# Making the queries of the second cross-attention for two tiles at once, in a loop body of sixteen steps

## The reference, cut to what matters

```python
B, S, D, H, DK, DV = (4, 256, 128, 16, 64, 64)
Q = (queries @ W_Q).reshape(b, sq, H, DK)
K = (keys @ W_K).reshape(b, skv, H, DK)
V = (values @ W_V).reshape(b, skv, H, DV)
scores = jnp.einsum('bqhd,bkhd->bhqk', Q, K)
scores = jnp.where(mask == 0, -jnp.inf, scores)
probs = jax.nn.softmax(scores * scaling, axis=-1)
attn = jnp.einsum('bhqk,bkhd->bqhd', probs, V).reshape(b, sq, H * DV)
return attn @ W_O
...
x = x + _L1_xattn_ref(_layernorm(x, axis=-1), ctx_1024, ctx_1024, mask_1x1xSxS2_ik0, ...)
```

## Time and profile before

| What | Value |
|---|---|
| median of 3 runs | 2666.25 us (2664.68 to 2667.53) |
| the profiled execution's own time | 2666.86 us |
| its span | 2665.0 us |
| TensorE busy | 2229.0 us, 84% of the span |
| VectorE busy | 1711.6 us, 64% |
| ScalarE busy | 1442.8 us, 54% |

### The profile page before, as it was taken

How to read it: one execution, slowest core, us unless ns; L and a number is a source line. 1 busy time by engine, 2 the same in 40 slices (tenths; PEclk the granted TensorE clock), 3 DMA queues, 4 the chain that set the end, 5 groups by cost and what they waited for, 6 DMA issues and landing times. The chain is left out here.

```text
span 2665.0 us, 80517 instructions
## 1 busy us (share of the span) xinstructions
PE 2229.0 (84%) x26087; PEld 1655.4 (62%) x26087; DVE 1711.6 (64%) x5620; ACT 1442.8 (54%) x3658; POOL 458.0 (17%) x1104
## 2 busy tenths in 40 slices
PE   5999999988759997999999999995357117499998
PEld 3777777767636665888888888884125103344444
DVE  4888888877654443777777777776789878701100
ACT  5888888876612223544554454453578747632221
POOL 2444444433213230000000000000000030000000
PEclk9999999999869997999999999998698555799999
DMA  3222222210100003444444444442000000100001
GB/s 92 75 73 73 73 73 73 73 38 1 26 0 0 0 0 92 113 109 106 113 109 104 106 116 104 108 110 71 0 0 0 0 1 4 45 0 0 0 0 32
DMA packets 257634, 140.91 MB, mean 53 GB/s; under 512 B 40176, under 2 KB 255616, under 8 KB 257152
## 3 DMA queue, kind: packets, MB, share of 16 engines
q1 hardware_dynamic: 257536, 139.61, 19.9%
HBM read 118.57 MB, written 20.97 MB: 52 GB/s over the span
## 5 line engine op out<-in xcount | busy, mean ns | idle before, releaser
L1075 DVE CUSTOM_DVE_ANT_0 c_SM<-c_bs,c_MB 128x257 f32<-128x257 f32 x512 | 211.1, 420 | 125.9 <-PE c_bs L979 124.2
L1052 ACT ACTIVATE c_OT<-c_bo 128x512 f32<-128x512 f32 x128 | 76.4, 597 | 389.5 <-PE c_bo L992 389.5
L979 PE MATMUL c_bs<-c_cT,c_QP 128*128 128x257 f32 x1024 | 264.1, 396 | 9.9 <-DVE c_LT L1094 9.9
L992 PE MATMUL c_bo<-c_PT,c_C 32*128 32x128 f32 x8192 | 266.0, 277 | 2.5 <-DVE c_PT L1090 2.3
L677 ACT ACTIVATE a_PR<-a_SM,a_nmx 128x257 f32<-128x257 f32 x512 | 253.4, 499 | 4.0 <-issue 3.3
L1046 ACT ACTIVATE c_PR<-c_SM,c_nmx 128x257 f32<-128x257 f32 x512 | 253.3, 504 | 0.0
L992 PEld LDWEIGHTS c_bo<-c_PT,c_C 32*128 32x128 f32 x8192 | 241.6, 187 | 18.6 <-issue 4.0
L979 PEld LDWEIGHTS c_bs<-c_cT,c_QP 128*128 128x128 f32 x1024 | 182.2, 190 | 56.6 <-issue 24.0
L724 DVE CUSTOM_DVE_ANT_0 a_SM<-a_bs,a_MB 128x257 f32<-128x257 f32 x512 | 187.9, 422 | 44.5 <-PE a_bs L545 38.6
L1090 DVE STREAM_TRANSPOSE c_PT<-c_PR 128x256 f32<-128x256 f32 x512 | 181.2, 411 | 0.0
L949 POOL TENSOR_TENSOR c_XL<-quarter,c_PR 128x16 f32<-128x16 f32 x128 | 27.6, 216 | 738.8 <-DVE c_PR L1085 738.8
(11 more groups left out here) (489 smaller groups left out, 4901.3 us busy)
## 6 DMA issues: line engine op xcount, KB each, us to landing
c_C<-in_ctx_dram SPq DMA_DIRECT2D x512, 128.0 KB, 2.8
a_C<-in_ctx_dram SPq DMA_DIRECT2D x128, 128.0 KB, 2.1
ctxT_dram<-a_cT SPq DMA_DIRECT2D x128, 128.0 KB, 1.9
c_cT<-ctxT_dram SPq DMA_DIRECT2D x128, 128.0 KB, 2.5
a_MK<-in_mask_Bx1xSxS_bk_dram SPq DMA_DIRECT2D x128, 32.1 KB, 1.9
X<-in_x_dram SPq DMA_DIRECT2D x4, 512.0 KB, 6.2
g_h<-in_L_ffn_h_w_dram SPq DMA_DIRECT2D x2, 1024.0 KB, 8.5
out_dram<-X SPq DMA_DIRECT2D x1, 2048.0 KB, 8.7
```

The costliest lines, as they stand in the source:

```text
L979: nc.tensor.matmul(b_s[hg][:, 0:SK], QP[:, r // 4 % 2, r % 4, 4 * hg:4 * hg + 4, :], cT[:, r, :], start=True, stop=True).then_inc(s_ps, 1)
L992: last = nc.tensor.matmul(b_o[:, h, 0:P], C[rows, buf, kb, :], PT[rows, s.r % 2, kb, :, :], start=(kb == 0), stop=(kb == NKB - 1), tile_po ...
L1075: nc.vector.tensor_tensor_reduce(SM[:, par, hg, :], b_s[hg][:, 0:SK], MB[:, :], 1.0, NEG1, ALU.add, ALU.max, mx[:, par, hg:hg + 1]).then_i ...
```

## The change

A pair of tiles (eight batches, 256 columns) takes the place of a tile in `queries`. A chunk is now two heads for a pair: 2 matmuls, 4 passes of 256 columns. Chunks alternate between banks 0 and 1 and banks 2 and 3 of `b_o`, in columns 128 to 383, and a chunk waits for the copy of the chunk before the last one, not of the last one. `QP` holds 2 x 8 batches in place of 2 x 4. There are still 128 chunks of 512 columns for ScalarE to copy; nine of them are made ahead of the steps, one in each step after that, and the last eight steps have none. The written-out steps are 16 at each end (with the three that finish), and the loop has 6 iterations of a body of 16 steps, on every engine; its branch is taken 5 times.

```diff
-        QP = sb("c_QP", [D, 2, BPT, H, SQ])
+        QP = sb("c_QP", [D, 2, 2 * BPT, H, SQ])
...
         def run(eng, step, extra):
 
-            def one(g, r, tile, fours, eights):
-                s = Step(g, r, B)
-                s.tile, s.fours, s.eights = tile, fours, eights
+            def one(g, r, first):
+                s = Step(g, r % 8, B)
+                s.fours, s.eights = (lambda lag: 4 * first + (r + lag) // 4), (lambda lag: 2 * first + (r + lag) // 8)
+                s.tile, s.side = s.fours(0), lambda lag: (r + lag) // 8 % 2
                 step(s)
-            for g in range(8):
-                one(g, g, g // 4, lambda lag, g=g: (g + lag) // 4, lambda lag, g=g: (g + lag) // 8)
-            with eng.Fori(1, B // 8 - 1) as j:
-                for r in range(8):
-                    one(8 * j + r, r, 2 * j + r // 4, lambda lag, j=j, r=r: 2 * j + (r + lag) // 4,
-                        lambda lag, j=j, r=r: j + (r + lag) // 8)
-            for g in range(B - 8, B + extra):
-                one(g, g % 8, g // 4, lambda lag, g=g: (g + lag) // 4, lambda lag, g=g: (g + lag) // 8)
+            for g in range(16):
+                one(g, g, 0)
+            with eng.Fori(1, B // 16 - 1) as j:
+                for r in range(16):
+                    one(16 * j + r, r, j)
+            for g in range(B - 16, B + extra):
+                one(g, g - (B - 16), B // 16 - 1)
...
-            def queries(tile, c, o_done):
-
-                wait(pe, q_ev, 4 * tile + c)
+            def queries(pair, c, o_done):
+
+                wait(pe, q_ev, 8 * pair + c - 1)
                 wait(pe, o_ev, o_done)
-                for i in range(4):
-                    last = nc.tensor.matmul(b_o[:, i, P:2 * P], A[:, 4 * c + i, :],
-                                            sh.XNT[:, ds(tile * P, P)], start=True, stop=True)
+                for i in range(2):
+                    last = nc.tensor.matmul(b_o[:, 2 * (c % 2) + i, P:3 * P], A[:, 2 * c + i, :],
+                                            sh.XNT[:, ds(pair * 2 * P, 2 * P)], start=True, stop=True)
                 last.then_inc(q_ps, 1)
...
-                if r % 4 == 0:
-                    wait(pe, q_ev, 4 * (s.tile + 1))
+                if r == 0:
+                    wait(pe, q_ev, 8 * (s.eights(0) + 1))
...
-                    nc.tensor.matmul(b_s[hg][:, 0:SK], QP[:, r // 4 % 2, r % 4, 4 * hg:4 * hg + 4, :], cT[:, r, :],
+                    nc.tensor.matmul(b_s[hg][:, 0:SK], QP[:, s.side(0), r, 4 * hg:4 * hg + 4, :], cT[:, r, :],
...
-                wait(pe, q_ev, g + 5 if s.on(-5) else B)
+                wait(pe, q_ev, g + 9 if s.on(-9) else B)
...
-                if s.on(-5):
-                    queries(s.fours(5), (r + 1) % 4, g - 2)
+                if s.on(-9):
+                    queries(s.eights(9), (r + 1) % 8, g - 2)
...
-            for c in range(5):
-                queries(c // 4, c % 4, 0)
+            for c in range(9):
+                queries(c // 8, c % 8, 0)
...
-            def queries(tile, par, c):
-                wait(act, q_ps, 4 * tile + c + 1)
-                wait(act, s_ps, 16 * (tile - 1))
-                nc.scalar.activation(QP[:, par, :, 4 * c:4 * c + 4, :].rearrange("p b h q -> p h b q"),
-                                     b_o[:, :, P:2 * P].rearrange("p h (b q) -> p h b q", b=BPT), ACT.Copy
-                                     ).then_inc(q_ev, 1)
+            def queries(pair, side, c):
+                wait(act, q_ps, 8 * pair + c + 1)
+                wait(act, s_ps, 32 * (pair - 1))
+                nc.scalar.activation(QP[:, side, :, 2 * c:2 * c + 2, :].rearrange("p b h q -> p h b q"),
+                                     b_o[:, 2 * (c % 2):2 * (c % 2) + 2, P:3 * P].rearrange(
+                                         "p h (b q) -> p h b q", b=2 * BPT), ACT.Copy).then_inc(q_ev, 1)
```

More of the change, by code:

```diff
@@ L1053, in step @@
                                          b_o[:, :, 0:P].rearrange("p h (a q) -> p h a q", a=4), ACT.Copy).then_inc(o_ev, 1)
[L1054 to L1058, removed]
+                if s.on(-9):
+                    queries(s.eights(9), s.side(9), (r + 1) % 8)
+            for c in range(9):
+                queries(c // 8, c // 8, c % 8)
             run(act, step, 2)
```

## The result

The changed kernel takes 2682.43 us (median of 4 runs, 2680.95 to 2683.86); the kernel before, run beside it, 2666.89 us. The ratio is 1.0059 with a 95% interval from 1.0042 to 1.0076: slower by 15.5 us, where 2680 us were forecast.

The account below looks back on a forecast made before the run. TensorE's own row of passes was taken to bound the loop. Savings of 8.4 us (2.3, 3.0, 2.5, 0.6) against 21.5 for code gave +13.1 on 2666.86: 2680 us, 0.5% slower, range 2660 to 2692.

Parts of the forecast that it names:

- The body's length: Loop: sixteen steps of code don't stay, so each of five taken branches costs 4.3 us (1.1 to 6.7), 21.5 in all.
- VectorE: Loop branch: its doubled body may have to fetch code too, but waits beside TensorE, not after it; no cost added.
- The chunk: Steps: four passes of 256 columns for eight of 128 save 0.026 us; three of four steps count, 2.3 us.
- The start: Ahead of the steps: nine chunks back to back, first scores after 10.7 us against 12.9, then at full clock; 3 us saved.
- The end: Last eight steps have no chunk, in place of the last four: 2.5 us saved, bounds 1.9 and 3.6.
- The loop's branch: Loop: taken 5 times, not 13; eight fewer at 0.07 us each save 0.6 us.
- the code stays: Rival: the new body's code stays in the engine, only savings are left, 2658 us; chance 0.18.
- it goes, but cheaply: Rival: code is fetched early or half covered, 1.7 us a branch, 2666 us, no change; chance 0.09.
- more hangs on it: Rival: a second packet and the low clock at each branch, 6 us a branch, 2688 us; chance 0.18.
- the slow start: Rival: clock stays low during the nine first chunks, 6 us on any case; 0.04 together with code that stays.

Follow-up runs that it names:

- e2: The kernel before, chunks of one tile, with only the loop body lengthened to 16 steps on all engines: 2692.31 us, ratio 1.0095.
- e4: The kernel before with a body of 16 steps on all engines but TensorE, which keeps 8: 2671.18 us, ratio 1.0018.
- e6: The changed kernel with VectorE, GpSimd and SyncE back at 8 steps, TensorE and ScalarE at 16: 2681.73 us, ratio 1.0059.
- e1: The changed kernel with TensorE's steps all written out, other engines looping over 16 steps: 2662.68 us, ratio 0.9983 to the kernel before.
- e5: The changed kernel with TensorE written out, VectorE, GpSimd and SyncE at 8 steps, ScalarE at 16: 2656.51 us, ratio 0.9968 to the kernel before.
- e8: Chunks of one tile, TensorE at 16 steps, others at 8, five of eight context blocks left out of the probabilities-context product (1760 TensorE records): 2625.39 us.
- e10: As the kernel with five context blocks left out, but with six of eight left out (1504 TensorE records): 2637.41 us.
- e3: The kernel before with TensorE's steps all written out, so that TensorE has no branch: 2668.16 us, ratio 1.0003.

## Why the prediction was right

*The body's length* was the step that decided, and it held. No row of before showed that sixteen steps of code don't stay, on which the 21.5 us rest: that was the author's estimate, and e2 shows it. The signs forecast were there: code that moves all along (13 packets in one round, 1342 to 1444 us, where some 11 were forecast), five waits before scores at "issue", the clock low (0.50) for 3.4 us after each. The sum had 3.1 + 1.2 = 4.3 us a branch; measured are 3.4 + 1.7 = 5.1. The landing of a small transfer and the packet's time, added, came 0.3 short. That a jump asks for its code only when it is taken shows too: a code packet starts about 1 us after each of the five branches does (the first at 1240.1, with none until 1241.0 and one between 1241.0 and 1241.2). The low clock followed each of the five, not two in three; the 1.9 us of one was near.

*VectorE* "may have to fetch", and "waits beside TensorE": both shown (e4, e6). That it costs about 1 us a branch once TensorE no longer waits (e1 against e5), the prediction didn't price; there was no need in the changed kernel.

*The chunk.* 0.026 us were forecast; the plain steps fell from 4.82 to 4.79 us in the trace, 0.03. The step before the tile's output fell from 5.25 to 5.22, and the output's step kept its 9.50: the c_LT wait takes that saving back, as worked out.

*The start.* 10.4 us to the first scores against 12.9, and 2.66 for the first step in place of 3.60: 3.4 us saved where 3 were forecast. Nine copies run under the chunks, and the clock rose early: 0.78 in this window against 0.50 in the same one before.

```profile
1048.00:1052.00 4.00, 4.00 (x16) 3.13 (x15) 0.00 (x0) 1.79 (x3) 0.00 (x0) 0.78 1.16 220
```

*The end.* The last eight steps, 119 to 127, take 43.5 us in place of 46.4: 2.9 saved, 2.5 forecast. The last four gained a little too.

*The loop's branch*: 0.6 forecast for eight branches. The 5.1 us above are counted against a step without any branch, so all 13 old ones count here, 1.0 us. And there is a gain that the sum had at nothing. Before, the tile's output at the head of each of the 14 bodies took 9.60 us in place of 9.51 (steps 10, 18, ...); after, only at the head of each of the six (18, 34, ...). In e5, where only ScalarE has a body of 16, it is also every sixteenth step, so it hangs on ScalarE's loop. Eight fewer save 0.7 us.

In all the phase gained 10.3 against the 8.4 of the sum. So both halves of the sum were too small, the cost by 15% (21.5 against 25.3) and the gain by 18%, and the errors went against each other: +13.1 forecast, +15.0 measured in the phase. That the total came so near is in part luck.

The rivals: "the code stays" fell by e2 and by the branch's record; "it goes, but cheaply" and "more hangs on it" lie on both sides of 5.1 us; the slow start didn't come.

How much code stays, the prediction's rows didn't show: they had the six packets of the old body, which stay, and nothing larger. 6.9 packets went (e8). The packets that the queue moved say more, as an estimate. Every packet has the same 16 KB, and a body that begins inside one lies in more of them than its size says. One more seems to be fetched ahead: a round of the changed kernel moved 13 packets for 11.4 packets of code (2908 records). In the first pass of the kernel before (1090 to 1144.5 us) and of e10 (1132 to 1230.8) the queue moved seven packets each:

```profile
q8 instruction: 7, 0.11, 0.8%
```

```profile
q8 instruction: 7, 0.11, 0.5%
```

With the one in which the body begins these are eight, the last of them ahead of its use, and both bodies stay. In e8 one round, from 1226.5 to 1321.5 us, moved nine, for its body goes:

```profile
q8 instruction: 9, 0.15, 0.9%
```

So eight packets of TensorE's code, the one ahead counted, are the most that these traces show to stay, and in e8, where a round moved nine, the body went. Whether this count is what decides stays open: a body of 6.9 packets that begins with a packet was not tried.

## What to carry to other kernels

Before a loop's body is made longer, count its records on each engine, and look in the trace whether instruction packets are moved inside the loop. Here the bodies that stayed had none (before and e10), and those that didn't paid at every taken branch: 5.1 us on TensorE in the changed kernel, whose phase it bounds (1.7 of them from the clock at 0.50 when it worked again), and about 1 us where VectorE alone waited (e1 against e5). Leave room: by the estimate above, the 5.9 packets of the old body were already eight. Here the cure was to write out the steps of that engine, since code in a row was free (e3: 2668.16 us, ratio 1.0003), and to lengthen the loop only on the engines that need it.

## What the runs showed of the hardware that was not expected

- A branch to code that is gone took 3.3 to 3.9 us on TensorE in the kernels with full work, and up to 4.9 in e8. On VectorE the wait was 2.8 us in e1 (2.2 in e4), it lay after the branch's record of 63 ns, and the views put it down to ScalarE.
- VectorE's body of 237 records stayed (e5: no code packet but TensorE's from 1250 to 1740 us) and that of 467 didn't (e4: 38 packets on the other engines' queue, five waits of 2.2 us).
- The kernel with the least work in the phase was not the fastest: e10 (2637.41 us, one run) has a third less in its values than e8 (2625.39, one run) and no wait at its branches, but its loop ran at a granted clock of 0.86, e8's at 0.97. These are windows of e8 and e10:

```profile
1350.00:1450.00 100.00, 88.41 (x856) 75.09 (x852) 78.10 (x326) 54.04 (x179) 6.59 (x36) 0.97 0.47 119
```

```profile
1350.00:1450.00 100.00, 92.53 (x708) 77.47 (x706) 75.58 (x317) 52.33 (x174) 6.22 (x34) 0.86 0.45 115
```
